# The last feed-forward layer of a decoder as one block over all four groups of sequences

## The reference

```python
def _conn_dense(kernel_bool, x):
    w = jnp.where(kernel_bool, jnp.float32(1.0), jnp.float32(-1.0))
    return x @ w
h = jnp.concatenate([x, -x], axis=-1)        # 256 -> 512
h = s0 * _conn_dense(k0, h)                  # -> 1024
h = jax.nn.relu(h) * 2
h = s1 * _conn_dense(k1, h)                  # -> 1024
h = jax.nn.relu(h) * 2
h = s2 * _conn_dense(k2, h)                  # -> 256
...
x = _layernorm(x + h)
```

## Time and profile before

| | us |
|---|---|
| median of three runs | 3654.58 |
| lowest, highest | 3645.28, 3659.48 |
| the profiled execution | 3658.22 |
| its span in the profile | 3656.4 |
| TensorE matmuls busy in the span | 2540.9 (69%) |
| VectorE busy | 1706.4 (47%) |
| ScalarE busy | 990.0 (27%) |
| GpSimd busy | 715.9 (20%) |
| the four calls of the last feed-forward part, first to last instruction | 3318.81 to 3646.01 |

### The profile page before, as it was taken

The page is one execution under the profiler, slowest core; times in us unless marked ns, Lnnn a source line. Parts: engine busy times, 40 slices in busy tenths (PEclk is TensorE's granted clock), DMA queues, the critical chain, the costliest instruction groups (busy, mean ns, idle before and its releaser), DMA issues. The chain is left out here.

```text
span 3656.4 us, 37516 instructions
## 1 busy us (share of the span) xinstructions
PE 2540.9 (69%) x14222; PEld 1636.6 (45%) x14270; DVE 1706.4 (47%) x3008; ACT 990.0 (27%) x1501; POOL 715.9 (20%) x497
## 2 busy tenths in 40 slices
PE   6886747762972764029946677795788987768877
PEld 4554424442861653028833455464333432344443
DVE  3544323342223345840056333323278999944454
ACT  2223222220111222202212323011365556422222
POOL 0000000003012001210020000303066667621211
PEclk9998878885995665559967888897899998888888
DMA  4020130003642000035510000245000000010000
GB/s 132 28 67 24 47 113 1 1 1 112 206 154 75 0 1 2 0 120 182 184 49 0 18 1 1 86 138 173 8 0 0 1 1 0 0 38 1 1 1 24
DMA packets 93442, 182.12 MB, mean 50 GB/s; under 512 B 8144, under 2 KB 79056, under 8 KB 87376
## 3 DMA queue, kind: packets, MB, share of 16 engines
q1 hardware_dynamic: 85584, 158.74, 12.9%
q0 software_dynamic: 7680, 20.98, 1.8%
HBM read 124.12 MB, written 55.57 MB: 49 GB/s over the span
## 5 line engine op out<-in xcount | busy, mean ns | idle before, releaser
L2475 POOL TENSOR_TENSOR l_attn_ring<-l_attn_ring,l_attn_c_rows 128x1024 f32<-128x1024 f32 x128 | 303.8, 2374 | 190.4 <-DVE l_attn_ring L2393 190.2
L2132 PE MATMUL bank<-l_attn_ring,identity 128*128 128x512 f32 x512 | 265.3, 643 | 71.0 <-POOL l_attn_ring L2475 58.0
L158 PE MATMUL bank<-x_features,weights 128*128 128x512 f32 x608 | 296.6, 637 | 24.5 <-issue 8.4
L2393 DVE TENSOR_TENSOR_SCAN l_attn_ring<-bank,l_attn_ring 128x512 f32<-128x512 f32 x256 | 299.2, 1210 | 21.1 <-ACT bank L2267 17.0
L2267 ACT ACTIVATE bank<-l_attn_step,l_attn_minus_exp_a_log 128x508 f32<-128x508 f32 x256 | 174.7, 686 | 236.7 <-DVE l_attn_ring L2393 228.5
L158 PEld LDWEIGHTS bank<-x_features,weights 128*128 128x128 f32 x608 | 123.3, 205 | 176.4 <-issue 161.1
L335 DVE TENSOR_REDUCE negmax_slots<-bank 128x16 f32<-128x2048 f32 x48 | 110.1, 2293 | 192.7 <-PE bank L270 192.7
L2132 PEld LDWEIGHTS bank<-l_attn_ring,identity 128*128 128x128 f32 x512 | 98.5, 201 | 197.1 <-issue 106.0
L2387 DVE TENSOR_TENSOR l_attn_ring<-l_attn_step_times_input,bank 128x1024 f32<-128x1024 f32 x128 | 154.2, 1205 | 47.7 <-POOL l_attn_step_times_input L2458 25.9
L2610 PE MATMUL bank<-l_ffn_hidden_parts,l_ffn_sign_weights 128*128 128x512 bf16 x752 | 165.6, 379 | 0.8
L149 PE MATMUL bank<-identity,x_tokens 128*128 128x128 f32 x256 | 55.9, 377 | 139.3 <-DVE x_tokens L197 137.9
(11 more groups left out here) (510 smaller groups left out, 4754.7 us busy)
## 6 DMA issues: line engine op xcount, KB each, us to landing
l_ffn_tile_weights<-l_ffn_experts SPq DMA_DIRECT2D x15, 2180.0 KB, 9.4
ffn_experts_tile_weights<-l_ffn_experts_experts SPq DMA_DIRECT2D x23, 1024.0 KB, 5.2
expert_slots<-zeros SPq DMA_DIRECT2D x8, 2048.0 KB, 7.5
l_ffn_tile_weights<-l_ffn_experts SPq DMA_DIRECT2D x23, 512.0 KB, 4.2
l_ffn_tile_x<-expert_slots SPq DMA_DIRECT2D x38, 256.0 KB, 2.7
expert_slots<-l_ffn_tile_y SPq DMA_DIRECT2D x38, 256.0 KB, 4.6
expert_slots<-zeros SPq DMA_DIRECT2D x1, 5888.0 KB, 18.8
l_ffn_experts_tile_x<-expert_slots SPq DMA_DIRECT2D x23, 256.0 KB, 2.7
```

Source lines behind the costliest of these rows:

```text
L158: mm = pe.matmul(out, w[:, f, m * P:(m + 1) * P], src[:, f, :], start=start and f == 0, stop=stop and f == k - 1)
L2132: mm = pe.matmul(net.banks[SUMS[j]][:], net.ident[:], ring[n % 4][:, j, :], start=s == 0, stop=s == STATES - 1)
L2393: nc.vector.tensor_tensor_scan(ring[n % 4][:, j, :], net.banks[DECAY[j]][:], ring[n % 4][:, j, :], 0.0, ALU.mult, ALU.add).then_inc(state_ ...
L2475: tt(ring[n % 4][:], ring[n % 4][:], c_row[:, n % STATES, :].unsqueeze(1).broadcast_to([P, 2, T]), ALU.mult).then_inc(out_ready, 1)
```

## The change

`l3_ffn` joins `WHOLE` and is called once. The tiles are numbered through all groups: 16g to 16g+7 for the first layer of group g, 16g+8 to 16g+15 for its second. The sign weights and scales are made once, during group 0. TensorE's order becomes first(0), second(0), first(1), third(0), second(1), first(2), third(1), and so on. All eight PSUM banks are used in turn, one for each tile of a layer; the third layer's output takes banks 0 and 1, in which tiles 4 and 5 lie, so it waits for the eviction of tile 5 of the next group's first layer, and the second half of the second layer waits for the statistics of the group before. ScalarE and VectorE go through the tiles in the order of their numbers; ahead of tile 16g+8 they split x of group g+1 and finish the output of group g-1. The output is stored by SyncE group by group inside the block (`store_out`), one transfer of 512 KB each; the last block only waits for the stores. Lines removed that the new ones replace are cut to "...":

```diff
-        bank = [2, 3, 4, 5, 2, 3, 4, 5, 0, 1, 6, 7, 2, 3, 4, 5]
+        Y = (0, 1)
+        def tile(layer, g, m):
+            return 16 * g + m if layer == 0 else 16 * g + 8 + m
+        def tile_of(n):
+            return (h0 if n // 8 % 2 == 0 else h1), n % 8
+        def bank(m):
+            return net.banks[(m + 4) % 8]
+        LAST = 16 * GROUPS
         with nc.Block() as block:
             @block.sync
             def _(sp):
                 prefetch(sp)
+                for g in range(GROUPS):
+                    sp.wait_ge(finish.x_ready, NB * (g + 1))
+                    net.store_out(sp, g)
             @block.tensor
             def _(pe):
+                def free(n):
+                    if n >= 8:
+                        pe.wait_ge(full_ready, n - 7)
+                def first(g):
+                    pe.wait_ge(x_high, g + 1)
+                    pe.wait_ge(x_middle, g + 1)
+                    pe.wait_ge(x_low, g + 1)
+                    for m in range(8):
+                        free(tile(0, g, m))
+                        for k in range(FT):
+                            for i, part in enumerate(xs.each):
+                                mm = pe.matmul(bank(m)[:], w0[:, k, m * P:(m + 1) * P], part[:, k, :],
+                                               start=k == 0 and i == 0, stop=k == FT - 1 and i == 2)
+                        mm.then_inc(h_in_psum, 1)
+                def second(g):
+                    for half_ in range(2):
+                        if half_ == 1 and g:
+                            pe.wait_ge(finish.var_ready, g)
+                        free(tile(1, g, 4 * half_ + 3))
+                        for k in range(8):
+                            if half_ == 0:
+                                pe.wait_ge(w1_ready, k + 1)
+                                pe.wait_ge(low_ready, tile(0, g, k) + 1)
+                                pe.wait_ge(middle_ready, tile(0, g, k) + 1)
+                            for m in range(4 * half_, 4 * half_ + 4):
+                                for i, part in enumerate(h0.each):
+                                    mm = pe.matmul(bank(m)[:], w1[:, k, m * P:(m + 1) * P],
+                                                   part[:, k, :], start=k == 0 and i == 0, stop=k == 7 and i == 2)
+                                if k == 7:
+                                    mm.then_inc(h_in_psum, 1)
+                def third(g):
+                    pe.wait_ge(full_ready, (tile(0, g + 1, 5) if g + 1 < GROUPS else tile(1, g, 5)) + 1)
+                    for b in range(NB):
+                        for k in range(8):
+                            if b == 0:
+                                pe.wait_ge(low_ready, tile(1, g, k) + 1)
+                                pe.wait_ge(middle_ready, tile(1, g, k) + 1)
+                            for i, part in enumerate(h1.each):
+                                mm = pe.matmul(half(net, Y, b), part[:, k, seq(b)], w2[:, k, :],
+                                               start=k == 0 and i == 0, stop=k == 7 and i == 2)
+                        mm.then_inc(y_ready, 1)
                 pe.wait_ge(w0_ready, 1)
...
+                first(0)
+                for g in range(GROUPS):
+                    second(g)
+                    if g + 1 < GROUPS:
+                        first(g + 1)
+                    if g == 0:
+                        pe.wait_ge(w2_ready, 1)
+                    third(g)
             @block.scalar
             def _(act):
...
+                def split_x(g):
+                    if g:
+                        act.wait_ge(h_in_psum, tile(0, g - 1, 7) + 1)
+                    nc.scalar.copy(xs.high[:], net.xT_all[:, g, :, :]).then_inc(x_high, 1)
+                    act.wait_ge(x_rest_ready, g + 1)
+                    nc.scalar.copy(xs.middle[:], x_rest[:]).then_inc(x_middle, 1)
+                split_x(0)
                 act.wait_ge(scale_ready, 1)
...
+                for n in range(LAST):
+                    h, m = tile_of(n)
+                    if n % 16 == 8 and n // 16 + 1 < GROUPS:
+                        split_x(n // 16 + 1)
+                    if n % 16 == 8 and n > 16:
+                        net.use(n // 16 - 1)
+                        finish.run_act(act, n // 16 - 1)
                     act.wait_ge(h_in_psum, n + 1)
                     if n >= 3:
                         act.wait_ge(rest_ready, n - 2)
...
+                    nc.scalar.activation(full[n % 3][:], bank(m)[:], ACT.Relu,
+                                         scale=scale[:, n // 8 % 2:n // 8 % 2 + 1]).then_inc(full_ready, 1)
                     act.wait_ge(full_ready, n + 1)
                     nc.scalar.copy(h.high[:, m, :], full[n % 3][:]).then_inc(high_ready, 1)
...
+                net.use(GROUPS - 1)
+                finish.run_act(act, GROUPS - 1)
             @block.vector
             def _(dve):
                 chain = Chain(dve, dve_steps)
...
+                def split_x(g):
+                    dve.wait_ge(x_high, g + 1)
+                    nc.vector.tensor_tensor(x_rest[:], net.xT_all[:, g, :, :], xs.high[:],
+                                            ALU.subtract).then_inc(x_rest_ready, 1)
+                    if g == 0:
+                        dve.wait_ge(net.ready["l3_ffn"], 16)
+                        nc.vector.tensor_tensor(w0, k0[:, 0:2, :], k0[:, 2:4, :], ALU.subtract).then_inc(w0_ready, 1)
+                    dve.wait_ge(x_rest_ready, g + 1)
+                    dve.wait_ge(x_middle, g + 1)
+                    nc.vector.tensor_tensor(xs.low[:], x_rest[:], xs.middle[:], ALU.subtract).then_inc(x_low, 1)
                 def remainder(n):
...
+                    h, m = tile_of(n)
                     dve.wait_ge(full_ready, n + 1)
                     dve.wait_ge(high_ready, n + 1)
                     if n >= 3:
@@ -2665,35 +2714,46 @@
                                             ALU.subtract).then_inc(rest_ready, 1)
                 def low(n):
...
+                    h, m = tile_of(n)
                     dve.wait_ge(rest_ready, n + 1)
                     dve.wait_ge(middle_ready, n + 1)
                     nc.vector.tensor_tensor(h.low[:, m, :], rest[n % 3][:], h.middle[:, m, :],
                                             ALU.subtract).then_inc(low_ready, 1)
...
+                def output(g):
+                    net.use(g)
+                    def add(b):
+                        dve.wait_ge(y_ready, NB * g + PAIR_DONE[b])
+                        ins = nc.vector.scalar_tensor_tensor(
+                            out=net.r[:, b, :], in0=half(net, Y, b), scalar=w["s2"], in1=net.x[:, b, :],
+                            op0=ALU.mult, op1=ALU.add)
+                        return ins
+                    finish.run_dve(dve, chain, add, g)
+                split_x(0)
+                chain(nc.vector.tensor_scalar(scale[:, 0:1], w["s0"], 4.0, None, ALU.mult))
+                nc.vector.tensor_scalar(scale[:, 1:2], w["s1"], 2.0, None, ALU.mult).then_inc(scale_ready, 1)
+                for n in range(LAST):
+                    if n % 16 == 8 and n // 16 + 1 < GROUPS:
+                        split_x(n // 16 + 1)
+                    if n % 16 == 8 and n > 16:
+                        output(n // 16 - 1)
                     remainder(n)
                     if n < 8:
                         nc.vector.tensor_scalar(w1[:, n, :], k1[:, n, :], 2.0, -1.0, ALU.mult,
                                                 ALU.add).then_inc(w1_ready, 1)
...
+                    if n % 8:
                         low(n - 1)
...
+                    if n % 8 == 7:
+                        low(n)
+                output(GROUPS - 1)
...
             @block.gpsimd
             def _(pool):
-                for n in range(16):
-                    h, m = (h0, n) if n < 8 else (h1, n - 8)
+                for n in range(LAST):
+                    h, m = tile_of(n)
                     pool.wait_ge(rest_ready, n + 1)
                     nc.gpsimd.tensor_copy(h.middle[:, m, :], rest[n % 3][:]).then_inc(middle_ready, 1)
...
-WHOLE = ("l0_ffn_experts", "l1_ffn", "l2_ffn", "l3_attn")
+WHOLE = ("l0_ffn_experts", "l1_ffn", "l2_ffn", "l3_attn", "l3_ffn")
...
+        def store_out(sp, g):
+            sp.dma_start(out[g * NB:(g + 1) * NB].rearrange("b t d -> t b d"),
+                         net.x_all[:, g * NB:(g + 1) * NB, :]).then_inc(out_stored, 16)
+        net.store_out = store_out
...
-                for n, view in enumerate(views(out, False)):
-                    sp.dma_start(view, net.x_all[:, n, :]).then_inc(out_stored, 16)
-                sp.wait_ge(out_stored, 16 * SEQUENCES)
+                sp.wait_ge(out_stored, 16 * GROUPS)
```

More of the change, by code:

```diff
@@ L2583, in _ @@
                 prefetch(sp)
+                for g in range(GROUPS):
+                    sp.wait_ge(finish.x_ready, NB * (g + 1))
+                    net.store_out(sp, g)
             @block.tensor
             def _(pe):
```

(18 more changed lines are left out.)

6 lines of the change are left out of this document (removed).

## The result

| | before | after |
|---|---|---|
| median, us | 3650.14 (3645.28 to 3659.48, 4 runs) | 3597.33 (3585.83 to 3599.10, 4 runs) |
| ratio | | 0.9846, 95% interval 0.9815 to 0.9876 |
| profiled execution, its span | 3658.22, 3656.4 | 3585.83, 3583.7 |
| first copy of x in the changed part | 3318.81 | 3310.27 |
| from there to the end of the span | 337.6 | 273.4 |

The forecast was 3594; 3597.33 was measured. In two later comparisons, on two chips, the same kernel had ratios of 0.9823 (0.9798 to 0.9848) and 0.9814 (0.9789 to 0.9840). The two profiled executions differ by more than the change: 8.5 of the 72.7 us lie ahead of the changed part.

What follows compares the result with a forecast made beforehand. TensorE was taken as the path within a call, the rest lying between its bursts. Periods 54.9 us plus stores 6.0 gave 60.9 us less: 3597.3 from the profiled execution, 3594 from the median; range 3580 to 3612.

Steps and rivals of the forecast that it cites:

- The period: One group's cycle on TensorE: 10.36 + 1.3 + 10.6 + 41.44 = 63.7 us against 81.99, saving 54.9 us over three.
- The hole: TensorE idle between next group's first layer and this group's third, awaiting tile 5's eviction: 1.3 us a group.
- T+7.1 for the last low part: T is when a group's second layer ends; VectorE's last low part of that layer ends 7.1 us later.
- the burst that gave the cadence: VectorE's remainder and low part in the earlier trace, 3380.71 to 3382.33 us: one tile per 1.62 us.
- The bound of 2.6 us: Upper bound of the wait before the third layer, if all tiles go at the 2.22 us cadence seen during weight conversions.
- The rival with a falling clock: TensorE's clock falls inside the dense block; 3781 us if at 1.2 GHz throughout; chance 5%.
- Cover for what was moved: Output, norm and split of x hide behind the second layer; output and statistics have some 16 us to spare.
- The stores: End of span: the last 512 KB store lands in 3.9 us; 4.4 us after last x instead of 10.4, 6.0 less.
- The last group: Last third layer and norm stay as before: the 7.15 us wait for parts and the cold clock remain.
- One block whose third layer stays late: Rival: only the holes between blocks go, third layer still takes 17.6 us; 44 us gain, 3611 us; chance 6%.
- The seam that stays half open: Rival: third layer waits for all 8 next first-layer tiles, 9.1 us later three times; 27 us more, 3621; chance 5%.
- The starting point: Median of three runs before the change, 3654.58 us, from which the forecast was counted; run spread -9/+5 us.

Runs made afterwards that it cites:

- conversions in every group: Changed kernel with VectorE converting the second layer's sign weights again in each group: block 278.4 us, 4.9 over the changed kernel; ratio to before 0.9853.
- in order: Changed kernel with each group's third layer ahead of the next group's first layer: block 292.1 us, 18.6 over the changed kernel; ratio to before 0.9877.
- third waits: Changed kernel whose third layer also waits until all 8 next first-layer tiles are split: block 309.6 us, 36.1 over the changed kernel; ratio to before 0.9897.
- tiles apart: Changed kernel with the four-tile loop outside in the second layer's second half: block 266.5 us, 7.0 under the changed kernel; ratio to before 0.9823.

## Why the prediction was right

- *The period.* 63.7 us forecast, 63.3 measured; three of them give 1.1 us of the 3.3 by which the block is shorter than forecast. The first and second layers were right to 0.1 us (10.36, 41.44). The third was said to take 10.6 and takes 10.5 to 10.7.
- *The hole.* 1.3 us forecast, 1.0 measured. The chain is the one that was named, the parts of it were right (T+7.1 for the last low part), but the remainders of tiles 0 and 1 took 1.28 us together and that of tile 2 0.68, where the burst that gave the cadence has 1.09 for each, and that of tile 2 ended at T+10.5, not T+11.0. Why they were quicker was not tested. The prediction's steps give 1.37 us (T+11.73 less T+10.36), which it rounded to 1.3. The bound of 2.6 us for conversions in every group was near: 1.9 in the run.
- *The clock.* The rival with a falling clock did not come: 1.00 over 240 us. The first and second layers are bf16 matmuls of 512 columns that cycle through all eight banks, and they ran at 1.00 in that stretch. TensorE is idle only three times in it, 0.8 us each, so this case says nothing of a stream with more idle time, as the one from 1188 to 1280 us of the kernel before (busy 78%, clock 0.63).
- *Cover for what was moved.* VectorE's and ScalarE's output and split of x hid behind the second layer; no second layer waited. There was less to spare than forecast: in the first such place VectorE ended the output at 3399.50 and then waited 12.4 us for the next tile, not some 16, because the output queued behind the split of x (ended at 3393.63).
- *The stores.* 6.0 us forecast, 7.1 measured. The step that was mis-sized is the landing of the last store: 3.9 us by the load of the same size, 2.9 in the trace.
- *The last group* was said to be as before; it is 1.1 us shorter: the third layer ran its last 75 matmuls in 9.49 us at a clock of 0.87 instead of 10.37 at 0.80, and they began at T+6.9 instead of T+7.15.
- *The rivals' prices.* One block whose third layer stays late was priced at 44 us of gain; run in order, it gained 45.5. The seam that stays half open was priced 27 us slower than the forecast; it cost 36, as the price left out that TensorE's clock fell in each of the waits of 10 us (2.2 to 2.5 us a group, and 1.3 in the last one).
- *The starting point* holds the largest uncertainty: the forecast was counted from a median of 3654.58, while medians of the kernel before in the later comparisons were 3632.39, 3661.68 and 3664.12, each on another chip. The ratio carries over (0.983 forecast), the microseconds don't. That the median came within 4 us of the forecast is partly luck: the two medians of the result are only 52.8 us apart, the interval allows 45 to 68, and by the block the gain is 64.2. The mechanism is borne out by the block and its terms, not by that nearness; all three terms that were off (periods, stores, last group) were off by 1.1 us to the same side.

Two places in the earlier parts make most of the 53 us by which the start of the block moves. From 1160 to 1420 us four like parts lie 56 to 65 us apart, with a mean granted clock of 0.63 in some profiles and 0.70 in another, and what follows begins up to 26 us earlier or later. And from the first to the last of the 48 gathers of expert outputs (1843.7 to 2558.3 us in the kernel before) 697 to 699 us pass in the four profiles taken on one chip, 714 to 717 in the eight others. Neither part is touched by the change. What decides the clock there stays open.

## What to carry to other kernels

TensorE ended the second layer with four tiles at once here, and the third layer's last 75 matmuls waited for the queue of their evictions until T+7.15 in the kernel before (T+6.9 in the last group of the changed kernel): put independent work of the next group there (18.6 us in all here), or let the tiles end apart (7.0 us more). Price such a hole from the slowest engine's cadence in the trace and the number of buffers; it came out within 0.3 us here. A wait of 10 us on TensorE cost the clock too: 0.80 to 0.82 in the layer behind it, which took 2.2 to 2.5 us more. And read a change of 1.5% in the stretch that it touches, when the rest of the kernel scatters by as much.

## What the runs showed of the hardware

- Through single gaps of 0.8 to 1.9 us the granted clock stayed at 1.00 (the third layer behind them took 10.64 us); in an idle time of 10 us on TensorE it came down each of three times (mean 0.72 to 0.75), and the next 96 matmuls of 256 columns took 12.8 to 13.2 us at 0.80 to 0.82.
- In the last group the same sparse batches (12, 3, 3, 3, with gaps of about 1 us) were followed by 75 matmuls in 9.47 to 9.49 us in all three profiles of the changed kernel, but in 11.27 and 11.28 us in two kernels that differ only before it (conversions in every group, in order), and 10.80 in a third (third waits). In the changed kernel the granted clock was 0.50 to 0.60 from T+6.9 to T+9.5 and 1.00 behind that; in the two slow ones it was 0.50 to 0.52 until about T+13. It repeats with the program and moves by 1.8 us with edits far ahead. It also differs between the groups of one run: in the kernel in order the four groups took 10.47, 9.99, 9.74 and 11.28 us. What decides it stays open.
- With only two gaps (0.85 and 0.77 us) in the last third layer, as with tiles apart, the clock stayed at 1.00 and the 75 matmuls took 8.36 us.
- A store of 512 KB from SBUF landed in 2.9 us, one of 128 KB in 1.8 us.
